# Windowed attention in one kernel with experts: softmax on merged blocks of 32 keys, and the weights split into an older block and a masked difference

## The chip, the cores and the metric

One core of a Trainium2 chip runs the whole program. The metric is the device time of one execution in microseconds, the median over runs. A profiled execution comes with its own time, which is its span in the trace plus a little around it.

## What is computed

```python
x  = L0_attn_x                       # (16, 256, 128), float32
xn = layernorm(x)
x  = x + attn_layer(xn) + experts(xn)

# attn_layer: 16 heads of 8, 4 key/value heads, window of 32
h = layernorm(x) * g1 + b1
q, k, v = h @ Wq + bq, h @ Wk + bk, h @ Wv + bv      # k, v repeated 4 times
q, k = rope(q), rope(k)
scores = einsum('bhqd,bhkd->bhqk', q, k) / sqrt(8)
valid  = (col <= row) & (row - col < 32)
attn   = softmax(where(valid, scores, -1e9))
out    = einsum('bhqk,bhkd->bhqd', attn, v)
x  = x + (out @ Wo + bo)
return x + gelu(layernorm(x) @ Wf1 + bf1) @ Wf2 + bf2   # with g2, b2

# experts: 8 of them, two for each token, hidden width 448
# inter = silu(x @ w1) * (x @ w3) * gate;  y = inter @ w2
```

## The kernel before

Every engine has its own program, written out in order; semaphores join them. A batch is 256 tokens, two tiles of 128. There are 16 batches and 8 blocks of 32 queries in each. `step(k)` of an engine holds what it does while batch k is in its scores: scores and shifted exponent for batch k, transposed weights, attend and norm for batch k-1, projection, residual and statistics for k-2, `h2` (the input of the feed-forward part) for k-3, and heads, keys and queries for k+1.

The program has four stretches. After normalisation and routing come the seven **lead steps** k = 0 to 6, in which POOL also issues 64 indirect DMAs that scatter the rows to the experts' slots, and VectorE also adds the bias and rotates queries and keys of batch k+2 (`add_bias`, `rotate`). Then come eight **expert steps** k = 7 to 14, each with nine expert tiles of 128 slots; here POOL does bias and rotation, and scatters each tile's result (`scatter_y`). A tile goes through `transpose_xs` (split), `take_xsT` on VectorE, `up_products` (seven products, 14 records in the trace, since a float32 product shows as two), `silu` on ACT, `gated` on VectorE (pair, L722, and two products, L728 and L730), `down_product` (four products) and `take_y` on ACT. `tile_up(i)` and `tile_down(i-1)` frame one slot of the order in which the attention work of TensorE stands. The up products of the next tile need the gate of the one before, since a tile uses the only pair of banks; a down product also waits for the split after the next. Last come step 15 and three more, in which the feed-forward part (`up`, `gelu`, `down`) and the sums of expert results (`add_experts`) run, with `resid` on POOL, and a tail of down products.

Scores of a batch before: four units of two blocks (`scores`, L1048 and L1053). Each block of 32 queries is multiplied with 64 keys, the older block and its own. Row partitions are (head of a group, query), columns (block, group g, keys). A bf16 product of the identity with a table of 0 and -1e30 puts the mask into PSUM first. `shift` takes the maximum out of PSUM (L650) and writes the difference to `S` (L657), `exps` works on all of `S` (L906), `weights_T` transposes a unit (L667), and `attend` (L1074) multiplies weights and values of both blocks, with four more columns for the sum. `norm` divides and transposes (L672 to L679). `newer`, `dv` and `pO` don't exist yet.

Other lines of the text: L894 and L900 take keys and queries to SBUF, L279 to L297 are bias and rotation, L412 and L415 the root for `h2` on POOL, L483 and L487 `resid` on POOL, L702 is `h2` on VectorE, L740 `add_experts`, L855 an early copy of 512 PSUM columns by ACT, L592 an early product of 512 columns on VectorE.

## Time and profile before

| | us |
|---|---|
| runs, median (lowest to highest) | 540.97 (540.45 to 542.07) |
| the profiled execution | 541.51 |
| its span | 539.6 |
| TensorE busy, products | 461.3 (85%) |
| VectorE busy | 380.3 (70%) |
| POOL busy | 252.5 (47%) |
| ACT busy | 232.4 (43%) |

A product's end is modelled, so starts are safer than ends on TensorE. The stretches by time: routing to about 54 us, lead steps to about 166, expert steps to about 452, the rest to 539.6. PE is TensorE's products, PEld its weight loads, DVE is VectorE.

### The profile page before, as it was taken

What the parts mean: (1) busy time and instruction counts of PE and PEld (TensorE: products, weight loads), DVE (VectorE), ACT (ScalarE), POOL (GpSimd) and SP (SyncE); (2) the same over time, 40 slices, a digit from 0 to 9 for tenths busy, and PEclk for the clock granted to TensorE, in tenths of its full rate; (3) what the DMA queues carried; (4) which work ended last, traced back from release to release, by engine and by line L of the source; (5) the groups of instructions that cost most, each with busy time, mean ns of one, the idle gap of its engine ahead of it and who ended that gap; (6) DMA issues with size and microseconds to landing.
All of it is one profiled execution on the core that took longest, in us unless ns stands there. A gap on an engine that the chain in (4) does not pass through costs nothing.

```text
span 539.6 us, 11287 instructions
## 1 busy us (share of the span) xinstructions
PE 461.3 (85%) x3102; PEld 408.8 (76%) x3103; DVE 380.3 (70%) x1132; ACT 232.4 (43%) x487; POOL 252.5 (47%) x373
## 2 busy tenths in 40 slices
PE   3921687898778999999999999999999998999967
PEld 2810476686668898888888998998988996675657
DVE  6868989779975847758578477584784753447784
ACT  2692433233251454445524544545335455454310
POOL 4626776744650734636437346363462425412520
PEclk9975777768777999999999999999999999999979
DMA  8961411100111455545544555454544540403042
GB/s 220 326 259 35 157 49 41 35 26 30 36 30 44 139 167 144 155 143 140 163 141 132 162 150 155 138 160 148 152 152 136 171 134 7 151 1 97 22 117 79
DMA packets 40571, 63.96 MB, mean 119 GB/s; under 512 B 6718, under 2 KB 27074, under 8 KB 40400
## 3 DMA queue, kind: packets, MB, share of 16 engines
q1 hardware_dynamic: 35456, 54.65, 33.3%
q0 software_dynamic: 4352, 8.47, 4.8%
q8 instruction: 23, 0.38, 0.3%
q10 hardware_dynamic: 720, 0.30, 0.3%
q14 instruction: 20, 0.16, 0.1%
HBM read 48.05 MB, written 15.87 MB: 118 GB/s over the span
## 4 chain that ended last, share of the span: by engine, by line
PE 57%; DVE 22%; issue 11%; ACT 8%; POOL 1%; DMA 1%; DVEq 0%; ACTq 0%; POOLq 0%
PE bank L1112 13%; PE bank L1074 11%; PE bank L1125 9%; PE bank L1053 6%; PE bank L1150 5%; PE bank L1139 4%; DVE rmax L650 3%; DVE pT L667 3%; DVE S L657 2%; PE bank L1086 2%; ACT L906 2%; DVE x_sb L740 2%; PE bank L1048 1%; DVE h L702 1%; ACT act L915 1%
## 5 line engine op out<-in xcount | busy, mean ns | idle before, releaser
L1112 PE MATMUL bank<-xsT,w_sb 128*128 128x128 f32 x1008 | 128.2, 279 | 4.4 <-DVE inter L730 2.7
L1112 PEld LDWEIGHTS bank<-xsT,w_sb 128*128 128x128 f32 x1008 | 119.5, 194 | 7.6 <-issue 5.4
L431 POOL DMA_INDIRECT scratch_ys<-ysb,pair x72 | 71.8, 997 | 36.1 <-issue 24.8
L1074 PEld LDWEIGHTS bank<-vbd,pT 128*128 128x128 f32 x512 | 73.7, 225 | 13.2 <-DVE pT L667 6.9
L1125 PE MATMUL bank<-w_sb,inter 128*128 x576 | 80.2, 282 | 4.1 <-issue 2.0
L1074 PE MATMUL bank<-vbd,pT 128*128 128x36 f32 x512 | 74.6, 303 | 10.3 <-DVE pT L667 9.2
L1125 PEld LDWEIGHTS bank<-w_sb,inter 128*128 128x128 f32 x576 | 71.8, 192 | 8.5 <-issue 7.0
L421 POOL DMA_INDIRECT scratch_xs<-xn_sb,slot x64 | 63.2, 988 | 31.5 <-issue 17.9
L243 POOL TENSOR_TENSOR spare_sb<-eps_sb 128x1 f32<-128x1 f32 x87 | 16.7, 192 | 128.0 <-ACT ysb L921 127.7
L1053 PE MATMUL bank<-kT,qbd 128*128 128x256 f32 x256 | 72.5, 410 | 0.0
L921 ACT ACTIVATE ysb<-bank 128x128 f32<-128x128 f32 x72 | 19.8, 275 | 114.8 <-PE bank L1125 114.8
L714 DVE COPY xsT<-bank 128x128 f32<-128x128 f32 x72 | 20.6, 286 | 67.2 <-PE bank L1101 66.9
L1053 PEld LDWEIGHTS bank<-kT,qbd 128*128 128x128 f32 x256 | 54.0, 211 | 8.8 <-issue 0.9
L650 DVE TENSOR_REDUCE rmax<-bank 128x4 f32<-128x256 f32 x128 | 47.0, 407 | 17.5 <-PE bank L1053 17.5
L657 DVE TENSOR_TENSOR S<-bank,rmax 128x256 f32<-128x256 f32 x128 | 48.3, 419 | 3.3
L667 DVE STREAM_TRANSPOSE pT<-S 128x512 f32<-128x512 f32 x64 | 44.4, 696 | 0.0
L894 ACT ACTIVATE kT<-bank 32x256 f32<-32x256 f32 x64 | 23.9, 373 | 41.7 <-PE bank L1037 41.2
L730 DVE TENSOR_TENSOR inter<-bank,act 128x384 f32<-128x384 f32 x72 | 40.1, 557 | 1.0
L906 ACT ACTIVATE S<-S 128x2048 f32<-128x2048 f32 x16 | 30.6, 1911 | 21.5 <-DVE S L657 21.4
L1048 PE MATMUL bank<-maskb_sb,identb_sb 128*128 128x512 bf16 x64 | 27.0, 422 | 11.7 <-DVE S L657 7.5
L1150 PEld LDWEIGHTS bank<-wf_sb,gT_sb 128*128 128x128 f32 x256 | 32.1, 207 | 5.9 <-issue 5.9
L914 ACT ACTIVATE act<-bank 64x128 f32<-64x128 f32 x72 | 19.3, 268 | 39.7 <-PE bank L1112 39.1
(136 smaller groups left out, 692.9 us busy)
## 6 DMA issues: line engine op xcount, KB each, us to landing
w_sb<-in_w SPq DMA_DIRECT2D x72, 448.0 KB, 3.3
scratch_xs<-blank_sb SPq DMA_DIRECT2D x9, 520.0 KB, 6.0
xsb<-scratch_xs SPq DMA_DIRECT2D x72, 65.0 KB, 1.8
w_sb<-scratch_ys SPq DMA_DIRECT2D x8, 512.0 KB, 5.2
w_sb<-in_w SPq DMA_DIRECT2D x1, 2048.0 KB, 10.9
out_dram<-x_sb SPq DMA_DIRECT2D x8, 256.0 KB, 2.3
scratch_ys<-ysb,pair POOLq DMA_INDIRECT x72, 2.6
scratch_xs<-xn_sb,slot POOLq DMA_INDIRECT x64, 2.3
```

What stands on the lines that cost most here:

```text
L421: nc.gpsimd.indirect_dma_start(xs, bass.IndirectOffsetOnAxis(ap=slot[:, t, c:c + 1], axis=0), xn_sb[:, t, :], None).then_inc(scattered[g], 16)
L431: nc.gpsimd.indirect_dma_start(ys, bass.IndirectOffsetOnAxis(ap=pair[:, i % 3:i % 3 + 1], axis=0), ysb[:, i % 3, :], None, bounds_check=2 ...
L650: last = nc.vector.tensor_reduce(rmax[:, u, n, :], src, AX.XY, ALU.max)
L657: last = nc.vector.tensor_tensor(S[:, u, n * 256:(n + 1) * 256].rearrange("p (h g k) -> p h g k", h=2, k=WIN), bank[u % 2][:, n * 256:(n + ...
L667: nc.vector.transpose(pT[:, 4 * u:4 * u + 4].rearrange("p n g q -> p (n g q)"), S[:, u, :]).then_inc(pT_ready, 1)
L730: nc.vector.tensor_tensor(inter[:, p, 0:FULL], h3_bank[:, 0:FULL], act1[:, p, 0:FULL], ALU.mult).then_inc(inter_ready, 1)
L906: nc.scalar.activation(S, S, ACT.Exp).then_inc(exp_ready, 1)
L1053: last = nc.tensor.matmul(bank[u % 2][:, i * 256:(i + 1) * 256], qbd[:, p, n].rearrange("p h q -> p (h q)"), kT[:, p, :, n * WIN:n * WIN + ...
L1074: last = nc.tensor.matmul(turn_bank[:, n * VW:(n + 1) * VW], pT[:, 2 * n + i].rearrange("p g q -> p (g q)"), vbd[:, p, n + i, :], start=(i ...
L1112: last = nc.tensor.matmul(to[:, c % EC * P:(c % EC + 1) * P], w13_sb[:, i % 3, c * P:(c + 1) * P], xsT[:, p, :], start=True, stop=True)
L1125: last = nc.tensor.matmul(y_bank[:, 0:D], inter[:, p, c * P:(c + 1) * P], w2_sb[:, ds(at + c * P, P)], start=(c == 0), stop=(c == EC - 1))
L1150: last = nc.tensor.matmul(bank[6 + i % 2][:, t * D:(t + 1) * D], gT[i % 4][:, c, t * P:(t + 1) * P], wf2_sb[:, c, :], start=(c == 0), stop ...
```

## The change

For each query 32 of the 64 keys are valid: of column j, the older block's key if j is above the query's place in its block, and the block's own key otherwise. The new kernel computes both blocks' scores for half a batch (four blocks) apart, own keys into bank 0 and older keys into bank 1, without a mask product; block 0 gets -1e30 as its older scores from one bf16 product. ACT copies the own scores to `S` (`keep_own`), VectorE copies older scores over them where the table `older` says so (`copy_predicated`), and takes maximum and difference in `S`. `S`, the exponential and the transposed weights `pT` are half as wide. For the values, each weight belongs to one of two keys: `attend` applies all weights to the older block's values and the weights times `newer` (`pO`, by `newer_part`) to the difference of own and older values (`dv`, by `value_steps`). `newer_part` runs on VectorE for batches 0 to 5 and on POOL after that, `value_steps` always on POOL. POOL's loop holds two steps in a turn in place of one, since the halves of the buffers alternate. POOL's bias and rotation stand behind one more scatter.

```diff
+        def in_lead(b):
+            return isinstance(b, int) and b < LEAD - 1
+        def part_count(b):
+            return (pO_ready_dve, b + 1) if in_lead(b) else (pO_ready, b + 2 - LEAD)
+        def newer_part(ops, eng, b):
+            ready = pO_ready_dve if in_lead(b) else pO_ready
+            eng.wait_ge(pT_ready, 2 * b + 2)
+            if some(b):
+                eng.wait_ge(pv_psum, b)
+            ops.tensor_tensor(pO.rearrange("p n g q -> p (n g) q"), pT.rearrange("p n g q -> p (n g) q"),
+                              bc(newer_sb.rearrange("p (a q) -> p a q", a=1), [P, NBLK * G, WIN]), ALU.mult).then_inc(ready, 1)
...
+            def value_steps(b, p):
+                pool.wait_ge(vbd_ready, b + 1)
+                if some(b - 1):
+                    pool.wait_ge(pv_psum, b - 1)
+                nc.gpsimd.tensor_tensor(dv[:, p, :, 0:NKV * HD], vbd[:, p, 1:NBLK + 1, 0:NKV * HD],
+                                        vbd[:, p, 0:NBLK, 0:NKV * HD], ALU.subtract).then_inc(dv_ready, 1)
...
+                if exists(k - 1) and not in_lead(k - 1):
+                    newer_part(nc.gpsimd, pool, k - 1)
                 if group is not None:
                     scatter(group, (0, 1))
                 tiles((0,))
...
                 if group is not None:
                     scatter(group, (2, 3))
                 tiles((1,))
+                if exists(k):
+                    value_steps(k, p)
+                tiles((2,))
                 if exists(k + 2) and not early(k + 2):
                     add_bias(nc.gpsimd, pool, k + 2)
                     rotate(nc.gpsimd, pool, k + 2)
-                tiles((2, 3, 4, 5, 6, 7))
+                tiles((3, 4, 5, 6, 7))
...
-            def shift(b, u):
-                dve.wait_ge(scores_psum, UNITS * b + u + 1)
...
-                last.then_inc(shifted, 1)
-            def weights_T(b, u):
+            def shift(b, h):
+                row = "p (a k) -> p a k"
+                half = S[:, h].rearrange(row, k=WIN)
+                dve.wait_ge(own_kept, 2 * b + h + 1)
+                wait_apart_dve("older_psum", older_psum, 2 * b + h + 1)
+                nc.vector.copy_predicated(half, bc(older_sb.rearrange("p (a k) -> p a k", a=1), [P, HALF * G, WIN]),
+                                          bank[1].rearrange(row, k=WIN)).then_inc(chosen, 1)
+                dve.wait_ge(chosen, 2 * b + h + 1)
+                nc.vector.tensor_reduce(rmax[:, h], half, AX.X, ALU.max).then_inc(rowmax_ready, 1)
+                dve.wait_ge(rowmax_ready, 2 * b + h + 1)
+                nc.vector.tensor_tensor(half, half, bc(rmax[:, h].rearrange("p (a k) -> p a k", k=1), [P, HALF * G, WIN]),
+                                        ALU.subtract).then_inc(shifted, 1)
+            def weights_T(b, h):
                 dve.wait_ge(exp_ready, b + 1)
                 if some(b):
                     dve.wait_ge(pv_psum, b)
-                nc.vector.transpose(pT[:, 4 * u:4 * u + 4].rearrange("p n g q -> p (n g q)"), S[:, u, :]).then_inc(pT_ready, 1)
+                    semaphore, value = part_count(b - 1)
+                    dve.wait_ge(semaphore, value)
+                nc.vector.transpose(pT[:, HALF * h:HALF * h + HALF].rearrange("p n g q -> p (n g q)"), S[:, h]).then_inc(pT_ready, 1)
...
+                    weights_T(k - 1, 1)
+                    if in_lead(k - 1):
+                        newer_part(nc.vector, dve, k - 1)
                 tile_split(2)
                 tile_gated(1)
-                if exists(k - 1):
-                    weights_T(k - 1, 1)
                 if exists(k):
                     values(k, p)
                 if exists(k + 1):
...
                 tile_split(3)
                 tile_gated(2)
                 if exists(k):
-                    shift(k, 1)
-                if exists(k - 1):
-                    weights_T(k - 1, 2)
+                    shift(k, 0)
                 tile_split(4)
                 tile_gated(3)
                 if exists(k - 3):
                     h2_of(k - 3)
-                if exists(k):
-                    shift(k, 2)
-                if exists(k - 1):
-                    weights_T(k - 1, 3)
                 tile_split(5)
                 tile_gated(4)
                 if exists(k):
-                    shift(k, 3)
+                    shift(k, 1)
...
+            def keep_own(b, h):
+                act.wait_ge(own_psum, 2 * b + h + 1)
+                if some(b):
+                    act.wait_ge(pT_ready, 2 * b)
+                nc.scalar.activation(S[:, h], bank[0], ACT.Copy).then_inc(own_kept, 1)
             def exps(b):
-                act.wait_ge(shifted, UNITS * b + UNITS)
+                act.wait_ge(shifted, 2 * b + 2)
                 nc.scalar.activation(S, S, ACT.Exp).then_inc(exp_ready, 1)
...
                 products(-1)
+                if exists(k):
+                    keep_own(k, 0)
                 gates(1)
                 products(0)
...
                 products(2)
+                if exists(k):
+                    keep_own(k, 1)
                 gates(4)
                 products(3)
...
-            def scores(b, p, u):
-                if u == 0:
+            def own_scores(b, p, h):
+                if h == 0:
                     pe.wait_ge(qbd_ready, b + 1)
                     pe.wait_ge(kT_ready, b + 1)
...
-                last.then_inc(scores_psum, 1)
+                if some(2 * b + h):
+                    pe.wait_ge(own_kept, 2 * b + h)
+                for i in range(HALF):
+                    n = HALF * h + i
+                    last = nc.tensor.matmul(bank[0][:, i * GW:(i + 1) * GW], qbd[:, p, n].rearrange("p h q -> p (h q)"),
+                                            kT[:, p, :, (n + 1) * WIN:(n + 2) * WIN], start=True, stop=True)
+                last.then_inc(own_psum, 1)
+            def older_scores(b, p, h):
+                if some(2 * b + h):
+                    pe.wait_ge(chosen, 2 * b + h)
+                for i in range(HALF):
+                    n = HALF * h + i
+                    if n == 0:
+                        last = nc.tensor.matmul(bank[1][:, 0:GW], identb_sb, neg_sb, start=True, stop=True)
+                    else:
+                        last = nc.tensor.matmul(bank[1][:, i * GW:(i + 1) * GW], qbd[:, p, n].rearrange("p h q -> p (h q)"),
+                                                kT[:, p, :, n * WIN:(n + 1) * WIN], start=True, stop=True)
+                last.then_inc(older_psum, 1)
...
             def attend(b, p, quarter, h2T_out):
                 if quarter == 0:
-                    pe.wait_ge(pT_ready, UNITS * b + UNITS)
-                    pe.wait_ge(vbd_ready, b + 1)
+                    semaphore, value = part_count(b)
+                    pe.wait_ge(semaphore, value)
+                    pe.wait_ge(dv_ready, b + 1)
                     if some(h2T_out):
                         pe.wait_ge(h2T_ready, h2T_out)
                 for n in range(quarter * NBLK // 4, (quarter + 1) * NBLK // 4):
-                    for i in range(2):
-                        last = nc.tensor.matmul(turn_bank[:, n * VW:(n + 1) * VW],
-                                                pT[:, 2 * n + i].rearrange("p g q -> p (g q)"),
-                                                vbd[:, p, n + i, :], start=(i == 0), stop=(i == 1))
+                    to = turn_bank[:, n * VW:(n + 1) * VW]
+                    if n > 0:
+                        nc.tensor.matmul(to, pT[:, n].rearrange("p g q -> p (g q)"), vbd[:, p, n, :], start=True, stop=False)
+                    last = nc.tensor.matmul(to, pO[:, n].rearrange("p g q -> p (g q)"), dv[:, p, n, :], start=(n == 0), stop=True)
                 if quarter == 3:
...
-                    scores(k, p, 0)
+                    own_scores(k, p, 0)
                 tile_down(-1)
                 tile_up(1)
                 if exists(k + 1):
...
                 tile_down(0)
                 tile_up(2)
                 if exists(k):
-                    scores(k, p, 1)
+                    older_scores(k, p, 0)
                 tile_down(1)
                 tile_up(3)
                 if exists(k):
-                    scores(k, p, 2)
+                    own_scores(k, p, 1)
                 tile_down(2)
                 tile_up(4)
                 if exists(k):
-                    scores(k, p, 3)
+                    older_scores(k, p, 1)
...
-    q, k = (p % WIN)[:, None], np.arange(KW)[None, :]
-    valid = (k - WIN <= q) & (k > q)
-    allowed = np.repeat(valid[:, None, :], NBLK, 1)
-    allowed[:, 0, :WIN] = False
-    maskadd = np.where(allowed, 0.0, NEG).reshape(P, -1).astype(f32)
+    older = (np.arange(WIN)[None, :] > (p % WIN)[:, None]).astype(np.int32)
+    newer = (np.arange(WIN)[None, :] >= (p % WIN)[:, None]).astype(f32)
```

VectorE, one lead step, from the norm of the batch before to the second (before) or last (after) shift. Before:

```order
L667 STREAM_TRANSPOSE pT<-S 128x512
L650 TENSOR_REDUCE rmax<-bank 128x4 x2
L657 TENSOR_TENSOR S<-bank,rmax 128x256 x2
L667 STREAM_TRANSPOSE pT<-S 128x512
L641 TENSOR_TENSOR vbd<-vt,vmask_sb 128x8x32
L540 STREAM_TRANSPOSE vt<-bank 128x256
L650 TENSOR_REDUCE rmax<-bank 128x4 x2
L657 TENSOR_TENSOR S<-bank,rmax 128x256 x2
L667 STREAM_TRANSPOSE pT<-S 128x512
L702 TENSOR_SCALAR h<-xn_sb,mv,rstd 128x128 x2
L650 TENSOR_REDUCE rmax<-bank 128x4 x2
L657 TENSOR_TENSOR S<-bank,rmax 128x256 x2
```

After:

```order
L704 STREAM_TRANSPOSE pT<-S 128x512 x2
L292 TENSOR_TENSOR pO<-pT,newer_sb 128x1024
L680 TENSOR_TENSOR vbd<-vt,vmask_sb 128x8x32
L577 STREAM_TRANSPOSE vt<-bank 128x256
L245 MEMSET spare_sb 128x1
L690 COPY_PREDICATED S<-older_sb,bank 128x512
L693 TENSOR_REDUCE rmax<-S 128x16
L695 TENSOR_TENSOR S<-S,rmax 128x512
L739 TENSOR_SCALAR h<-xn_sb,mv,rstd 128x128 x2
L245 MEMSET spare_sb 128x1
L690 COPY_PREDICATED S<-older_sb,bank 128x512
L693 TENSOR_REDUCE rmax<-S 128x16
```

Both transposes now stand in a row at the head, the product with `newer` behind them, and the shifts are two groups of copy, maximum and difference in place of four pairs.

ACT, head of the expert loop's first step (two tiles: SiLU of tile 0, take_y of the last tile, SiLU of tile 1). Before:

```order
L914 ACTIVATE act<-bank 64x128
L915 ACTIVATE act<-bank 128x384
L920 ISA
L921 ACTIVATE ysb<-bank 128x128
L911 REGISTER_ALU
L914 ACTIVATE act<-bank 64x128
L915 ACTIVATE act<-bank 128x384
L920 REGISTER_ALU
L921 ACTIVATE ysb<-bank 128x128
```

After:

```order
L952 ACTIVATE act<-bank 64x128
L953 ACTIVATE act<-bank 128x384
L958 ISA
L959 ACTIVATE ysb<-bank 128x128
L937 ISA
L940 ACTIVATE S<-bank 128x512
L949 REGISTER_ALU
L952 ACTIVATE act<-bank 64x128
L953 ACTIVATE act<-bank 128x384
```

The copy of the own scores (L940) stands between the first tile's result and the second tile's SiLU.

POOL, head of the same step: scatter of the last tile, scatter of tile 0, then the root for h2. Before:

```order
L243 TENSOR_TENSOR spare_sb<-eps_sb 128x1
L431 DMA scratch_ys<-ysb,pair 8192x128
L429 REGISTER_ALU
L243 TENSOR_TENSOR spare_sb<-eps_sb 128x1
L431 DMA scratch_ys<-ysb,pair 8192x128
L411 ISA
L412 TENSOR_TENSOR ve<-mv,eps_sb 128x2
L413 REGISTER_ALU
L415 TENSOR_TENSOR rstd<-ve,nhalf_sb 128x2
```

After:

```order
L249 TENSOR_TENSOR spare_sb<-eps_sb 128x1
L454 DMA scratch_ys<-ysb,pair 8192x128
L289 ISA
L292 TENSOR_TENSOR pO<-pT,newer_sb 128x1024
L452 REGISTER_ALU
L249 TENSOR_TENSOR spare_sb<-eps_sb 128x1
L454 DMA scratch_ys<-ysb,pair 8192x128
L434 ISA
L435 TENSOR_TENSOR ve<-mv,eps_sb 128x2
L436 REGISTER_ALU
L438 TENSOR_TENSOR rstd<-ve,nhalf_sb 128x2
```

The product with `newer` (L292) stands ahead of tile 0's scatter and of the root.

## Rows read from the trace of the kernel before

**Rows 1.** The page, part 4: the chain that ended last, by engine.

```profile
PE 57%; DVE 22%; issue 11%; ACT 8%; POOL 1%; DMA 1%; DVEq 0%; ACTq 0%; POOLq 0%
```

**Rows 2.** Busy time by stretch, one in the lead, one in the expert steps.

```profile
92.00:109.00 17.00, 14.43 (x64) 12.49 (x64) 13.85 (x41) 5.38 (x10) 9.72 (x12) 0.70 0.10 32
...
250.00:286.00 36.00, 33.96 (x270) 31.71 (x270) 24.19 (x71) 17.11 (x39) 16.86 (x29) 1.00 0.50 148
```

**Rows 3.** Groups by line and shape: busy us, mean ns, idle before.

```profile
L657 DVE TENSOR_TENSOR S<-bank,rmax 128x256 f32<-128x256 f32 x128 | 48.3, 419 | 3.3
...
L650 DVE TENSOR_REDUCE rmax<-bank 128x4 f32<-128x256 f32 x128 | 47.0, 407 | 17.5 <-PE bank L1053 17.5
...
L667 DVE STREAM_TRANSPOSE pT<-S 128x512 f32<-128x512 f32 x64 | 44.4, 696 | 0.0
...
L906 ACT ACTIVATE S<-S 128x2048 f32<-128x2048 f32 x16 | 30.6, 1911 | 21.5 <-DVE S L657 21.4
...
L592 DVE TENSOR_TENSOR h2T_sb<-h2T_sb 128x512 f32<-128x512 f32 x1 | 0.7, 691 | 0.0
...
L483 POOL TENSOR_TENSOR x_sb<-x_sb,bf_sb 128x512 f32<-128x512 f32 x8 | 10.3, 1288 | 0.0
...
L855 ACT ACTIVATE xnT<-bank 128x512 f32<-128x512 f32 x8 | 4.8, 600 | 3.8 <-PE bank L996 3.8
```

**Rows 4.** Timeline, lead steps: start, us, engine, line, operation.

```profile
67.58 0.70 DVE L667 STREAM_TRANSPOSE pT<-S 128x512 f32<-128x512 f32 x1
...
99.22 0.67 DVE L667 STREAM_TRANSPOSE pT<-S 128x512 f32<-128x512 f32 x1
...
102.98 1.57 ACT L900 ACTIVATE qbd<-bank,qmask_sb 128x256 f32<-128x256 f32 x4
...
107.82 3.22 PE L1074 MATMUL bank<-vbd,pT 128*128 128x36 f32 x16 [1.56 <-DVE pT L667]
...
116.57 0.67 DVE L667 STREAM_TRANSPOSE pT<-S 128x512 f32<-128x512 f32 x1
...
131.49 0.67 DVE L667 STREAM_TRANSPOSE pT<-S 128x512 f32<-128x512 f32 x1
...
165.24 0.45 DVE L679 STREAM_TRANSPOSE outT<-on 128x256 f32<-128x256 f32 x1
```

**Rows 5.** Timeline of one expert step, 250 to 287 us.

```profile
252.04 0.38 PE L1048 MATMUL bank<-maskb_sb,identb_sb 128*128 128x512 bf16 x1
...
252.45 0.87 POOL L279 TENSOR_TENSOR qkb<-gT_sb,bqkv_sb 128x320 f32<-128x320 f32 x1
...
252.52 0.83 DVE L722 SCALAR_TENSOR_TENSOR pair<-xsb,slotgrid_sb 128x1 int32<-128x1 f32 x1
...
253.12 1.05 PE L1125 MATMUL bank<-w_sb,inter 128*128 x8
...
254.36 1.64 PEld L1112 LDWEIGHTS bank<-xsT,w_sb 128*128 128x128 f32 x14 [0.38 <-issue]
...
257.75 0.20 DVE L722 SCALAR_TENSOR_TENSOR pair<-xsb,slotgrid_sb 128x1 int32<-128x1 f32 x1
...
258.96 1.64 PEld L1112 LDWEIGHTS bank<-xsT,w_sb 128*128 128x128 f32 x14
...
265.82 1.91 ACT L906 ACTIVATE S<-S 128x2048 f32<-128x2048 f32 x1
...
266.02 1.64 PEld L1112 LDWEIGHTS bank<-xsT,w_sb 128*128 128x128 f32 x14
...
271.12 1.64 PEld L1112 LDWEIGHTS bank<-xsT,w_sb 128*128 128x128 f32 x14
```

**Rows 6.** The chain in order of time: start us, us, what.

```profile
198.24 0.97 PE bank L1125 x8
...
447.16 0.97 PE bank L1125 x8
```

**Rows 7.** Timeline, the step after the last batch.

```profile
487.83 0.63 DVE L702 TENSOR_SCALAR h<-xn_sb,mv,rstd 128x128 f32<-128x128 f32 x2
```

93 lines of the change are left out of this document (40 added, 53 removed).

## The prediction, made before the change was run

> **What bounds the kernel now.** The chain that ended last comes first: TensorE holds 57% of it and VectorE 22% [rows 1], so two kinds of stretch have to be told apart. The busy table by stretch does that [rows 2]. From 92 to 109 us, in the seven lead steps, VectorE works 13.9 of 17 us at a TensorE clock of 0.70. From 250 to 286 us, in the eight steps that also run nine expert tiles each, TensorE is busy 34 of 36 us at full clock (the 2.4 GHz level). The lead is paced by VectorE with waits of VectorE and TensorE on each other; the expert steps are paced by TensorE, with gaps where it waits for what ACT and VectorE make of each tile.
>
> A lead step in order of time [rows 4]: the first weight transpose of a step starts at 99.22 and that of the next at 116.57, 17.35 us. TensorE can't begin to apply the weights (attend, L1074) before the fourth transpose, at 107.82, which is 8.6 us into the step; once begun, norm, the last VectorE work of the step, waits for it. Six such steps, from 67.58 to the end of the last output transpose at 165.69, take 98.1 us, 16.4 each. They differ with TensorE's clock: attend's first 16 records take 3.22 us at 107.82, at the low level, and the step after 116.57, with the clock risen in its second half, takes 14.92 in place of 17.35.
>
> Expert steps: from 198.24 to 447.16 seven of them pass, 35.6 us each [rows 6]. Inside one, the starts of the up products of following tiles lie 4.60 us apart at 254.36 and 258.96, and 5.10 apart at 266.02 and 271.12 [rows 5]. Work alone doesn't fill these: 14 records of up take 1.64 us, so one record of 128 columns costs 0.117; up, down, split and eight more records are 31, or 3.6 us. In the first of these intervals VectorE is late: shifts, transposes and h2 stand between the gates, and a scalar_tensor_tensor on 128x1 takes 0.83 us at 252.52 beside POOL's L279. In the second ACT is late: the exponential on 2048 columns runs from 265.82 for 1.91 us, between two table loads, and the SiLU of the tile stands behind it.
>
> **The change, part by part.** *Scores on TensorE.* Before, a unit is one mask product on 512 bf16 columns and two products on 256; it starts at 252.04 and the next work at 253.12, so four units cost 4.32 us a batch. After, 15 products on 128 columns are 30 records, 3.5 us, and one bf16 product about 0.1. Attend goes from 16 products to 15, 0.23 less. Together 0.95 us a batch, where TensorE is the bound.
>
> *VectorE's softmax.* Before, by the means [rows 3], eight maxima at 0.407, eight subtractions at 0.419 and four transposes at 0.696 are 9.4 us. After, two predicated copies, two maxima and two subtractions on 512 columns, and two transposes. No row shows a predicated copy. The nearest rows are the 512 column products, 0.69 (L592), for two streams that are each read once; the far end is four passes, 2.8 us. I take 0.69, because mask and data are again two streams and the kept value is not needed. The maximum on 512 comes by the same slope to 0.68. That is 2 x (0.69 + 0.68 + 0.69) + 2 x 0.70 = 5.5 us. Three operations that follow each other by a semaphore, and one memset for the wait, give back about 0.2 each half.
>
> *The masked part of the weights.* 1024 columns on VectorE in the lead: from 0.419 at 256 and 0.691 at 512 it is 1.2 us. On POOL, where 512 columns take 1.29 (L483), 2.4 to 2.6 us. *Value steps*, 256 columns on POOL, half of L483, about 0.7.
>
> *ACT.* Two new copies of 512 PSUM columns at 0.60 (L855) are 1.2 us; the exponential halves from 1.91 to about 1.05. Work is even, but it moves out of the place where it hurts.
>
> **Lead steps.** VectorE saves 9.4 - 5.5 - 1.2 - 0.4 = 2.3 us by the means; single pairs before overlap a little, so I take 1.9. The path says the same: attend no longer waits for four transposes mixed with shifts but for both transposes at the step's start, the mask product, and h2, which TensorE transposes first: 1.4 + 1.2 + 0.85 for values and their transpose + 2.2 for one shift + 0.6 for h2 + 0.5 to TensorE's transpose is about 6.8, against 8.6. Second shift, bias, rotation, residual and norm follow as before. Six steps at 1.9 are 11, and the first step, with shifts only, 1; together 12 us. The new ACT copy of the second half stands behind keys and queries (each as long as the 1.57 us at 102.98) and ends at about 5.8, before VectorE wants it at 6.3. POOL works 9.7 us in 17 and gets 0.7 more; with the pauses between its scatters that is some 13 and stays below the 14.5 that remain. Bounds: if all six steps find the low clock, they take 6 x (17.35 - 1.9) = 93, and 5 + 1 = 6 us are gained; if all find the high one, 14.92 - 1.9 = 13.0, of which VectorE's own work, now without a wait, gives back up to 0.5, and the gain is 18 us.
>
> **Expert steps.** Interval by interval. (a) The three that hold scores in front of a down product get 0.14 shorter each by records, 0.5 us, of which 0.2 are hidden where ACT's keys and queries hold the SiLU. (b) The interval of 4.60: after the gate only h2 is left on VectorE, and POOL's rotation, moved behind one more scatter, doesn't meet h2 any more; TensorE's own work is 3.6 + 0.25, so 0.75 goes. (c) The interval before it loses one transpose and one shift of two, 0.3. (d) The interval of 5.10 is set by ACT and loses what the exponential loses, 0.86. (e) Where attend has three products instead of four, VectorE's chain takes over, 0.1. The sum is 2.3. Against it stand meetings with POOL: the subtraction now has both inputs in SBUF, as the pair instruction (L722) has, and stands next to POOL's rotation. The 0.83 us at 252.52, against 0.20 for the same instruction at 257.75, show the price of one meeting, 0.6; half of it a step, 0.3. So 2.0 us, eight steps, 16 us. The new wait in ACT's queue (copy of the first half, behind both transposes, ahead of the second tile's SiLU) costs 0.1 to 0.7 on ACT; heads and a down product on TensorE cover it, with about 0.3 to spare. POOL's 2.5 us product ends some ten microseconds before attend asks for it. The values product on VectorE may wait for it about 1.9 us, and the wait for the next split covers that. Bounds: 0.7 a step, when only the TensorE records are saved and some of them are lost again, 6 us; 3 a step, 24.
>
> By the Trainium skill (SBUF — State Buffer, Who interferes with whom) a VectorE instruction with two SBUF inputs and a GpSimd instruction that reads SBUF exclude each other for a whole instruction. By that rule the trace agrees: the instruction of 252.52 ends at 253.35 and POOL's L279 at 253.32 [rows 5]. The rule speaks against this change, since POOL's new product is 2.5 us long; the first rival works that out from rows.
>
> **Tail.** The last batch's scores and the weights of the batch before save 1.1 us, and the exponential 0.9. But in the step after the last batch POOL has the mask product ahead of rstd, and h2 waits for rstd. Before, h2 starts at 487.83 [rows 7]; now it stands behind transposes that end near 486.5, 2.5 of product and about 0.9 of rstd, at 489.9, 2.1 late, which eats the 2.0; 1 more for POOL's product meeting the expert sums on VectorE. Net +1, from -2 to +3.
>
> **Sum.** The profiled execution took 541.5 us (span 539.6), the median of the runs is 540.97. 541.5 - 12 - 16 + 1 = 514.5. All parts at their poor ends give 541.5 - 6 - 6 + 3 = 532.5, all at their good ends 541.5 - 18 - 24 - 2 = 497.5; they rarely fall so together, and the forecast's own range is 503 to 528.
>
> **Rivals.** *Meetings with POOL eat the expert steps.* POOL now has 3.2 us more of SBUF reads a step, one of them 2.5 us long; if VectorE's values, pair or subtraction stand behind it and the next gate is late, each step loses 1 to 2 us of its 2.3. For it: 252.52. Against it: the product begins after the scatter of the last tile, when VectorE mostly waits for a split. Expert steps -4, lead -9 and tail +3 give 531.5. *The predicated copy is slow, and the kernel ends slower than before.* Place: in the middle of each shift, 14 times on the lead's VectorE path and 16 times between two gates. Every microsecond over 0.69 costs about 30; from 0.69 + 27/30 = 1.6 us a copy the gain is gone; at four passes, 2.8, the time is 514.5 + 63 = 577. For it: no row. Against it: every VectorE operation in the rows keeps to about 1.06 ns a column. *The lead finds the low clock everywhere*, since TensorE does less work: lead -6 in place of -12, 520.5; inside the forecast's range. *More than forecast*: all lead steps at the high clock and 3 us an expert step give 541.5 - 18 - 24 + 1 = 500. *The change saves TensorE nothing*, because narrow products cost as much as wide ones: against it, 14 records of 128 columns take 1.64 us, and a unit with four records on 256 takes 1.08 with its mask.
>
> **How the numbers follow.** Forecast with the low clock case inside 0.68, meetings with POOL 0.20, slow copy 0.07, more than forecast 0.05. The predicted time is 514.5. The range 501 to 532 takes in the case of POOL's meetings, and leaves out the slow copy, the most of the more-than-forecast case and the edges of the others, somewhat under 2 in 10. A measurement of this kernel tells a change from none at about 0.3%, 1.6 us. Faster: the three cases under 533 and their edges, 0.91; the same 0.02; slower: 0.07.
>
> **What would show it.** Right: COPY_PREDICATED near 0.7 us; lead steps of 14 to 15.5 us; expert steps near 33.6; the exponential near 1.05 and the interval across it near 4.2; gaps of TensorE behind VectorE's gates smaller. Wrong: a copy above 1.6 us; the second tile's SiLU waiting for the first copy of S; VectorE's values, pair or subtraction of 2 us beside POOL's product; attend waiting for POOL; lead steps that stay at 16 us with VectorE idle before norm.

## The result, and the profile after

The kernel got slower. Four runs of the changed kernel have a median of 557.7 us (551.89 to 560.54), those of the kernel before beside them 540.71 (539.51 to 542.07): a ratio of 1.028, interval 1.019 to 1.037. Ratios and their intervals, here and below, are of fast executions alone (here 560.54 is left out as slow), so they differ a little from the quotients of the medians. The forecast was 514.5, the range 501 to 532.

The profiled execution took 551.89 us, the fastest of the four, with a span of 550.0. From the page of the changed kernel, its engines and its chain by engine, which answer to [rows 1]:

```profile
span 550.0 us, 11471 instructions
...
PE 448.4 (82%) x3246; PEld 411.2 (75%) x3247; DVE 370.1 (67%) x979; ACT 236.0 (43%) x519; POOL 303.7 (55%) x401
...
PE 49%; DVE 23%; issue 13%; POOL 7%; DMA 5%; ACT 2%; DVEq 0%; POOLq 0%; ACTq 0%
```

TensorE's share of the chain fell from 57% to 49%, and two names that had 1% each hold 12% now: POOL and a DMA. The groups of the changed kernel by line and shape (columns as in [rows 3]):

```profile
L759 DVE SCALAR_TENSOR_TENSOR pair<-xsb,slotgrid_sb 128x1 int32<-128x1 f32 x72 | 44.0, 611 | 13.6 <-DMA scratch_ys<-ysb,pair 13.4
...
L695 DVE TENSOR_TENSOR S<-S,rmax 128x512 f32<-128x512 f32 x32 | 24.2, 757 | 1.1
L292 POOL TENSOR_TENSOR pO<-pT,newer_sb 128x1024 f32<-128x1024 f32 x10 | 23.6, 2359 | 26.1 <-DVE pT L704 25.9
L690 DVE COPY_PREDICATED S<-older_sb,bank 128x512 f32<-128x512 int32 x32 | 23.3, 729 | 19.8 <-PE bank L1104 19.2 <-issue 0.6
L693 DVE TENSOR_REDUCE rmax<-S 128x16 f32<-128x512 f32 x32 | 22.0, 686 | 1.1
L704 DVE STREAM_TRANSPOSE pT<-S 128x512 f32<-128x512 f32 x32 | 20.5, 679 | 0.0
L940 ACT ACTIVATE S<-bank 128x512 f32<-128x512 f32 x32 | 19.2, 600 | 45.8 <-DVE pT L704 43.0 <-PE bank L1091 2.7
...
L944 ACT ACTIVATE S<-S 128x1024 f32<-128x1024 f32 x16 | 16.9, 1057 | 11.9 <-DVE S L695 11.8
```

Every new operation costs about what the prediction gave it: predicated copy 0.729 us (0.69 forecast), maximum 0.686 (0.68), subtraction 0.757 (0.69), GpSimd's product 2.36, exponential 1.06. What stands out is the first row. The pair instruction works on one column a partition and takes 0.20 us when nothing disturbs it; its mean is now 0.61, over 72 of them, and before it 13.6 us are spent on a DMA that nobody waited for before, but once for 0.6 us.

By stretch, from the timelines of the two profiled executions: the first up product of the expert steps starts at 155.19 (165.92 before), 10.7 earlier; from there to the start of the last down product are 302.2 us (286.2), 16.0 more; from there to the end 92.6 (87.5), 5.1 more. The sum is +10.4, and 541.5 + 10.4 is 551.9.

Inside an expert step, the starts of the up products of its nine tiles (0 to 8) cut it into nine intervals. I read the starts from TensorE's timeline and took means over six steps, the second to the seventh. This ruler serves for every kernel below (us; those left out stay within 0.5 of each other):

```
kernel                                1-2   3-4   4-5   5-6   6-7   7-8   step  low clock
before                                3.70  4.16  4.59  3.64  3.47  5.14  35.83   0
after                                 5.81  3.94  3.89  3.71  5.40  4.22  37.87   3
rot_back                              5.81  3.95  3.75  5.66  4.14  4.31  38.24   3
mask_dve                              3.74  4.00  4.00  3.71  5.46  4.80  36.74   4
both                                  3.77  5.11  3.75  4.78  4.07  4.11  36.59   2
pieces                                3.79  4.08  3.93  3.70  5.26  4.70  36.41   2
before_load                           5.43  4.36  4.59  3.72  3.47  5.14  37.69   0
before_load4                          3.68  4.07  4.61  3.72  3.47  5.12  35.82   0
pieces_late                           3.80  4.82  3.75  3.91  3.80  4.20  35.22   1
dve_late                              3.77  4.95  3.75  3.55  3.58  4.21  34.86   0
dve_rot2                              3.78  3.53  4.31  3.70  5.24  4.83  36.40   3
dve_split                             3.78  4.85  4.25  3.40  3.56  4.21  35.12   0
whole_late                            5.81  4.64  3.75  5.23  4.53  4.43  39.28   4
before_rot                            3.68  3.72  4.31  3.53  5.25  4.25  35.89   2
```

The last column counts the places in all eight expert steps where the granted clock fell, the low clock with which the first step begins in every kernel aside. In the kernel before there are none. The second row against the first is the result in one line: 4-5 and 7-8 lost 0.70 and 0.92 as forecast, and 1-2 and 6-7 gained 2.11 and 1.93.

**The interval 1-2: VectorE held by GpSimd.** Timeline of the changed kernel, 198.5 to 203 us:

```profile
198.64 2.78 DVE L759 SCALAR_TENSOR_TENSOR pair<-xsb,slotgrid_sb 128x1 int32<-128x1 f32 x1
199.03 2.36 POOL L292 TENSOR_TENSOR pO<-pT,newer_sb 128x1024 f32<-128x1024 f32 x1
201.45 0.29 DVE L765 TENSOR_TENSOR inter<-bank,act 64x128 f32<-64x128 f32 x1
201.75 0.56 DVE L767 TENSOR_TENSOR inter<-bank,act 128x384 f32<-128x384 f32 x1
...
202.46 0.79 PE L1163 MATMUL bank<-xsT,w_sb 128*128 128x128 f32 x5 [1.89 <-DVE inter L767]
```

The pair instruction of tile 1, 0.20 us of work, ends at 201.42, and GpSimd's product at 201.39. The gate stands behind it in VectorE's queue and TensorE behind the gate: 1.89 us idle here, 0.92 in the first step and 1.9 to 2.4 in the others.

**The interval 6-7: a scatter that leaves late.** The same kernel, 211 to 224 us:

```profile
211.75 0.89 POOL L300 TENSOR_TENSOR qkb<-gT_sb,bqkv_sb 128x320 f32<-128x320 f32 x1
...
213.88 0.28 ACT L959 ACTIVATE ysb<-bank 128x128 f32<-128x128 f32 x1 [2.10 <-PE bank L1176]
...
216.31 0.72 POOL L318 TENSOR_TENSOR kr<-ra,rb 128x256 f32<-128x256 f32 x1
...
217.34 1.01 POOL L454 DMA_INDIRECT scratch_ys<-ysb,pair  x1 [0.15 <-POOL spare_sb L249]
...
217.77 0.33 SPq L351 DMA_DIRECT2D w_sb<-in_w  x1
...
221.70 0.22 DVE L759 SCALAR_TENSOR_TENSOR pair<-xsb,slotgrid_sb 128x1 int32<-128x1 f32 x1 [2.05 <-DMA scratch_ys<-ysb,pair]
...
222.96 1.24 PE L1163 MATMUL bank<-xsT,w_sb 128*128 128x128 f32 x9 [1.86 <-DVE inter L767]
```

The result of tile 3 is ready at 214.16, but GpSimd is in bias and rotation until 217.03, which now stand behind the scatter of tile 2; the scatter goes out at 217.34. The pair of tile 6 uses the same of three buffers and must wait for it to land; it starts 4.36 us after the issue. VectorE waits 2.05, TensorE 1.86. The wait has two parts: the scatter leaves late, and it also takes 4.2 us to land, where the scatters of this kernel take a median of 2.8. The row of L351, a load of weights on SyncE's queue, comes back under whole_late.

**The clock.** Busy time by stretch of the changed kernel (columns as in [rows 2]), two steps, and three pieces of 4 us in the second:

```profile
230.46:268.05 37.59, 32.96 (x283) 31.85 (x281) 24.19 (x60) 17.25 (x41) 21.18 (x31) 1.00 0.50 142
268.05:308.96 40.91, 36.23 (x283) 34.70 (x281) 24.16 (x60) 17.27 (x41) 20.66 (x31) 0.92 0.44 129
...
274.00:278.00 4.00, 2.02 (x15) 1.60 (x14) 3.89 (x5) 1.83 (x6) 3.71 (x4) 1.00 0.21 78
278.00:282.00 4.00, 3.89 (x23) 3.85 (x24) 1.98 (x6) 0.78 (x3) 1.39 (x3) 0.65 0.49 148
282.00:286.00 4.00, 4.00 (x35) 4.00 (x35) 2.76 (x8) 2.50 (x7) 1.66 (x3) 0.93 0.42 131
```

TensorE is busy 2.02 of 4 us before 278, where the pair of tile 1 is held, and then the granted clock is 0.65: part of the stretch at the 1.2 GHz level. The step with two such falls has the same records and takes 3.3 us more than its neighbour. Not every wait of 1.9 us is followed by a fall.

**The tail.** Timeline of the changed kernel, the step after the last batch, against [rows 7]:

```profile
491.45 2.34 POOL L292 TENSOR_TENSOR pO<-pT,newer_sb 128x1024 f32<-128x1024 f32 x1 [17.82 <-DVE pT L704]
493.75 0.19 POOL L435 TENSOR_TENSOR ve<-mv,eps_sb 128x2 f32<-128x2 f32 x1
494.02 0.71 POOL L438 TENSOR_TENSOR rstd<-ve,nhalf_sb 128x2 f32<-128x2 f32 x1
494.76 2.06 DVE L739 TENSOR_SCALAR h<-xn_sb,mv,rstd 128x128 f32<-128x128 f32 x2 [3.39 <-POOL rstd L438]
...
496.93 0.66 PE L1113 MATMUL bank<-ident_sb,h 128*128 128x128 f32 x2 [4.97 <-issue]
```

`h2` starts 37.4 us after the last down product of the expert steps (35.8 before), takes 2.06 in place of 0.63 beside GpSimd's next products, and TensorE stands idle for 4.97 us. The clock follows. Busy time by stretch, the 20 us that begin 30 us after that last down product, in the changed kernel and then in the kernel before:

```profile
487.35:507.35 20.00, 14.28 (x51) 8.30 (x50) 11.14 (x29) 7.63 (x11) 6.45 (x7) 0.74 0.23 66
```

```profile
482.07:502.07 20.00, 18.89 (x107) 13.57 (x106) 13.84 (x46) 9.21 (x12) 5.01 (x8) 0.91 0.25 78
```

TensorE gets 51 records through in place of 107, at a granted clock of 0.74 in place of 0.91.

By the Trainium skill (SBUF — State Buffer, Who interferes with whom) a VectorE instruction with two SBUF inputs contends with a GpSimd instruction that reads SBUF, and whichever comes first holds the shared ports for its whole length while the other waits. The trace agrees on the length: 2.78 us of the pair beside 2.36 of the product, with ends 0.03 apart. It doesn't agree on the order, as far as recorded starts tell: the pair's begins 0.39 us ahead of the product's, and the pair is the one that waits.

### The profile page after: what moved, and what is told of

Read it like the earlier page. It is cut to its first block, busy times and chain, and to the rows that moved or that the text cites. A ratio compares the mean times of both kernels' runs of the same rounds, so it can differ in the third digit from the quotient of the medians.

```text
span 550.0 us, 11471 instructions
## 1 busy us (share of the span) xinstructions
PE 448.4 (82%) x3246; PEld 411.2 (75%) x3247; DVE 370.1 (67%) x979; ACT 236.0 (43%) x519; POOL 303.7 (55%) x401
## 4 chain that ended last, share of the span: by engine, by line
PE 49%; DVE 23%; issue 13%; POOL 7%; DMA 5%; ACT 2%; DVEq 0%; POOLq 0%; ACTq 0%
PE bank L1163 15%; PE bank L1176 7%; DMA scratch_ys<-ysb,pair 5%; PE bank L1201 5%; PE bank L1127 4%; PE bank L1190 4%; PE bank L1126 3%; PE bank L1091 3%; PE bank L1104 3%; DVE inter L767 2%; DVE pT L704 2%; DVE x_sb L777 2%; PE bank L1137 2%; DVE S L690 1%; DVE xn_sb L560 1%
## 5 line engine op out<-in xcount | busy, mean ns | idle before, releaser
L1127 PE MATMUL bank<-dv,pO 128*128 128x36 f32 x256 | 54.6, 299 | 3.7 <-ACT h2T_sb L917 3.7
L759 DVE SCALAR_TENSOR_TENSOR pair<-xsb,slotgrid_sb 128x1 int32<-128x1 f32 x72 | 44.0, 611 | 13.6 <-DMA scratch_ys<-ysb,pair 13.4
L1127 PEld LDWEIGHTS bank<-dv,pO 128*128 128x128 f32 x256 | 44.6, 218 | 5.4 <-issue 5.4
L1091 PE MATMUL bank<-kT,qbd 128*128 128x128 f32 x256 | 41.8, 316 | 5.3 <-ACT qbd L932 3.5
L1126 PE MATMUL bank<-vbd,pT 128*128 128x36 f32 x224 | 45.9, 291 | 0.0
L1091 PEld LDWEIGHTS bank<-kT,qbd 128*128 128x128 f32 x256 | 38.2, 228 | 7.6 <-issue 7.1
L1126 PEld LDWEIGHTS bank<-vbd,pT 128*128 128x128 f32 x224 | 39.2, 218 | 1.1 <-issue 1.0
L940 ACT ACTIVATE S<-bank 128x512 f32<-128x512 f32 x32 | 19.2, 600 | 45.8 <-DVE pT L704 43.0
L292 POOL TENSOR_TENSOR pO<-pT,newer_sb 128x1024 f32<-128x1024 f32 x10 | 23.6, 2359 | 26.1 <-DVE pT L704 25.9
L690 DVE COPY_PREDICATED S<-older_sb,bank 128x512 f32<-128x512 int32 x32 | 23.3, 729 | 19.8 <-PE bank L1104 19.2
L1104 PE MATMUL bank<-kT,qbd 128*128 128x128 f32 x224 | 35.4, 303 | 1.4 <-DVE S L690 1.4
```

The lines of the kernel that those rows point to most:

```text
L690: nc.vector.copy_predicated(half, bc(older_sb.rearrange("p (a k) -> p a k", a=1), [P, HALF * G, WIN]), bank[1].rearrange(row, k=WIN)).then ...
L759: nc.vector.scalar_tensor_tensor(pair[:, b:b + 1], xsb[:, b, D + 1:XW], slotgrid_sb[:, ds(j, 1)], xsb[:, b, D:D + 1], ALU.is_equal, ALU.ad ...
L1091: last = nc.tensor.matmul(bank[0][:, i * GW:(i + 1) * GW], qbd[:, p, n].rearrange("p h q -> p (h q)"), kT[:, p, :, (n + 1) * WIN:(n + 2) * ...
L1104: last = nc.tensor.matmul(bank[1][:, i * GW:(i + 1) * GW], qbd[:, p, n].rearrange("p h q -> p (h q)"), kT[:, p, :, n * WIN:(n + 1) * WIN], ...
L1126: nc.tensor.matmul(to, pT[:, n].rearrange("p g q -> p (g q)"), vbd[:, p, n, :], start=True, stop=False)
L1127: last = nc.tensor.matmul(to, pO[:, n].rearrange("p g q -> p (g q)"), dv[:, p, n, :], start=(n == 0), stop=True)
```

## The experiments

All ratios are against runs of the kernel before on the same chip. Four kernels first undo one thing of the change each.

**rot_back.** The rotation goes back to its old place, value steps before it.

```diff
                 if exists(k):
                     value_steps(k, p)
-                tiles((2,))
                 if exists(k + 2) and not early(k + 2):
                     add_bias(nc.gpsimd, pool, k + 2)
                     rotate(nc.gpsimd, pool, k + 2)
-                tiles((3, 4, 5, 6, 7))
+                tiles((2, 3, 4, 5, 6, 7))
```

> The changed kernel with one thing undone: POOL's bias and rotation stand again ahead of the scatter of tile 2. Theory A (two new waits cost the expert steps, POOL's product with newer and the late scatter of tile 3): the wait of VectorE's pair instruction for the DMA of scratch_ys, 13.4 us in the changed kernel, falls under 3 us; TensorE's gap of 1.9 us before the up product of tile 8 goes; 8 x 1.9 less, some 535 to 548 us. Rival (the scatter's place doesn't matter, the waits come from the halves of S and ACT's queue): within 2 us of the changed kernel.

556.84 us median, ratio 1.028 (1.020 to 1.036): nothing gained, a miss. The number is the one that the rival named, but its mechanism (halves of `S`, ACT's queue) isn't in the trace. The ruler says why nothing was gained: the wait didn't go, it moved from 6-7 to 5-6 (5.66). Now the scatter of tile 2 stands behind 0.75 us of value steps and 4.9 of bias and rotation. The pair of tile 5 asks for it 1.1 us after its issue and waits 1.8 to 3.3 us. Before, with the rotation alone in that place, the margin had been just enough.

**mask_dve.** The product for the masked part on VectorE for all batches.

```diff
         def in_lead(b):
-            return isinstance(b, int) and b < LEAD - 1
+            return True
```

> The changed kernel with the product with newer on VectorE for all batches, nothing else moved. Theory A: pair (L759) beside that product falls from 2.6 to 0.2 us, TensorE's gap of 1.9 us before the up product of tile 2 falls under 0.5 since 1.2 us of VectorE work take its place; 8 x 1.4 less in the expert steps and about 4 less after the last batch, where POOL's root for h2 waited: 536 to 545 us. Rival (POOL's extra work as such is what costs, by late scatters): the DMA wait would shrink and the gap before tile 2 stay.

537.06 us (534.63 to 538.22), ratio 0.989 (0.981 to 0.996). Interval 1-2 is 3.74 again. VectorE does 1.22 us more a step, and the kernel is 20 us faster than with that work on GpSimd.

**both.** Both edits together.

> Both edits: rotation ahead of tile 2's scatter, product with newer on VectorE. Theory A: the expert steps come near the 33.6 us of the prediction plus what 1.2 us of VectorE work cost, and the time is 515 to 530 us, faster than the kernel before. If one wait only hides behind the other, the sum of the two single gains isn't reached and the time stays above 535.

538.58 us (530.46 to 541.49), ratio 0.996 (0.992 to 1.000): a miss by 9 us, with the wait again in 5-6. What came is the other branch of the expectation, one wait behind the other and a time above 535. The profiled execution, 528.6 of span, was the fastest; it has two falls of the clock and a mean granted clock of 0.910; the two slowest, 541.0 and 541.5, have 0.896. So the spread of this kernel goes with the clock.

**pieces.** The product stays on GpSimd, cut in four.

```diff
-            ops.tensor_tensor(pO.rearrange("p n g q -> p (n g) q"), ...
+            pieces = 1 if in_lead(b) else 4
+            step = NBLK // pieces
+            for i in range(pieces):
+                at = slice(i * step, (i + 1) * step)
+                last = ops.tensor_tensor(pO[:, at].rearrange("p n g q -> p (n g) q"), ...
+            last.then_inc(ready, 1)
```

> The changed kernel with POOL's product with newer in four pieces of 256 columns in place of one of 1024, same place, somewhat more POOL time (4 x 0.72 against 2.36). Theory A with an exclusive hold for one instruction: pair waits for one piece only, 0.9 us in place of 2.6, and TensorE's gap before tile 2 falls from 1.9 to about 0.3: 8 x 1.4 less, 539 to 548 us. Rival (VectorE is slowed for as long as POOL works, whatever the pieces): no change, 550 to 560.

537.24 us (535.68 to 539.05), ratio 0.989 (0.982 to 0.997). GpSimd works more (2.8 to 3.0 us in place of 2.36), and 20 us are gone all the same. So it isn't GpSimd's work that costs, but that it comes in one long instruction. The gain is even larger than expected. The pair was to wait for one piece, 0.9 us; it takes 0.82 in the last two steps, but only 0.21 to 0.48 in the second to the sixth. In the second it begins 0.39 us ahead of the first piece, as far as it began ahead of the whole product in the rows above, and here it isn't held to the piece's end. Why the same head start helps against the short instruction and not against the long one stays open.

Then the same from the other side: the kernel before, with idle work added.

**before_load.** In each expert step GpSimd multiplies 1024 columns that nobody reads.

```diff
                 if some(0 if m is None else m):
                     tiles((-1,))
+                if m is not None:
+                    pool.wait_ge(pT_ready, UNITS * (k - 1) + 1)
+                    nc.gpsimd.tensor_tensor(loadB, loadA, loadA, ALU.mult)
```

> The kernel before, with one idle product added to GpSimd in each expert step: 1024 columns f32, SBUF to SBUF, after the scatter of the last tile of the step before, waiting for the first weight transpose as the new mask product does. Nobody reads its result. Theory A (an SBUF instruction of GpSimd holds back VectorE's instructions with two SBUF inputs, the pair above all, until it ends): the pair instruction there takes over 2 us, TensorE waits about 1.9 us a step, and the low clock follows in some steps: 15 to 22 us in all, 555 to 563. Rival B (the price in the changed kernel came from its other waits, and the product alone is covered): 540 to 543.

556.31 us (554.13 to 557.96), ratio 1.026 (1.021 to 1.032). The timeline, 244 to 256 us:

```profile
248.46 2.34 DVE L728 SCALAR_TENSOR_TENSOR pair<-xsb,slotgrid_sb 128x1 int32<-128x1 f32 x1
248.86 1.91 POOL L456 TENSOR_TENSOR loadB<-loadA 128x1024 f32<-128x1024 f32 x1
...
251.84 1.80 PE L1118 MATMUL bank<-xsT,w_sb 128*128 128x128 f32 x14 [1.43 <-DVE inter L736]
```

The same picture as in the changed kernel, alone: interval 1-2 is 5.43 in place of 3.70, the step 1.9 us longer, and the clock stays full in the second to the eighth step. One idle instruction a step on an engine that is busy half of the time costs 13.5 us.

**before_load4.** The same work in four instructions of 256 columns.

```diff
-                    nc.gpsimd.tensor_tensor(loadB, loadA, loadA, ALU.mult)
+                    for at in range(0, 1024, 256):
+                        nc.gpsimd.tensor_tensor(loadB[:, at:at + 256], loadA[:, at:at + 256], loadA[:, at:at + 256], ALU.mult)
```

> The same idle product cut into four of 256 columns, about 0.72 us each, 2.9 us in all on GpSimd. Theory A: the pair waits for one piece at most, 0.7 us a step in place of 2: 541 to 547. If it is GpSimd's time as such that costs (its scatter comes later by the sum), it is as slow as the product in one piece or slower.

542.59 us, ratio 1.001 (0.995 to 1.007). No difference. The timeline, 236 to 250 us:

```profile
240.73 0.47 DVE L729 SCALAR_TENSOR_TENSOR pair<-xsb,slotgrid_sb 128x1 int32<-128x1 f32 x1
241.24 2.52 POOL L457 TENSOR_TENSOR loadB<-loadA 128x256 f32<-128x256 f32 x4
241.54 0.56 DVE L737 TENSOR_TENSOR inter<-bank,act 128x384 f32<-128x384 f32 x1
```

2.5 us on GpSimd cost nothing; 1.9 us in one instruction cost 13.5. The pair ends at 241.20, just ahead of the first piece, so here no piece holds it. The gate (L737) has one input in PSUM and runs at 0.56 in the midst of them.

Next, the second cause: value steps and rotation apart.

**pieces_late.** Rotation at its old place, value steps behind the scatter of tile 5, product in pieces.

```diff
                 tiles((1,))
-                if exists(k):
+                if m is None and exists(k):
                     value_steps(k, p)
                 ...
                     rotate(nc.gpsimd, pool, k + 2)
-                tiles((2, 3, 4, 5, 6, 7))
+                tiles((2, 3, 4, 5))
+                if m is not None and exists(k):
+                    value_steps(k, p)
+                tiles((6, 7))
```

> The changed kernel with GpSimd's mask product in four pieces (537.2 before), the rotation ahead of the scatter of tile 2 again, and the value steps moved from ahead of the rotation to behind the scatter of tile 5, in the expert steps. Theory C (what is left in each step is one wait of 1.3 to 2.2 us of the pair for a scatter that GpSimd issues late, because value steps and rotation together, or the rotation one tile later, stand ahead of it; the kernel before has a margin of under 0.75 us there): the wait goes, 1.5 to 2 us a step, and with it the low clock of single stretches: 518 to 526. Rival D (the scatters fly longer for another reason, traffic of the weight loads): 535 to 539.

532.14 us (526.35 to 540.43), ratio 0.978 (0.970 to 0.986), a miss by 6 us. The ruler shows the DMA's wait gone from four steps of six, with 3.3 in 5-6, and still there in two (5.18 and 4.95); theory C is right as far as it goes, but the margin is not safe.

**dve_late.** The same with the product on VectorE.

> The same with the mask product in one piece on VectorE. Theory C: 516 to 525. Rival D: 535 to 539, as the kernel with the product on VectorE and the rotation moved back had it (538.6).

519.24 us (518.23 to 520.71), ratio 0.958 (0.953 to 0.963). A hit, and the fastest kernel of all: 38 us less than the changed one with the same arithmetic. TensorE's waits for the gate are mostly gone and no expert step behind the first has a low clock:

```profile
PE 442.0 (86%) x3246; PEld 405.7 (79%) x3247; DVE 370.3 (72%) x989; ACT 236.0 (46%) x519; POOL 284.1 (55%) x391
...
PE 63%; DVE 18%; issue 8%; ACT 5%; DMA 3%; POOL 1%; DVEq 0%; POOLq 0%; ACTq 0%
```

(Page of dve_late, engines and chain.) Against both, it moves nothing but the value steps, 0.75 us a step, to where GpSimd waits anyway; that is worth 19 us.

**dve_rot2.** As dve_late, but the rotation where the change had put it, behind the scatter of tile 2.

> As the kernel at 519.2 (product on VectorE, value steps behind the scatter of tile 5), but with the rotation behind the scatter of tile 2, where the change had put it. It differs from the kernel at 537.1 by the place of the value steps alone. Theory C1 (the rotation one scatter later is enough to make a scatter late): the interval of the up products of tiles 6 and 7 is again near 5.4 us in place of 3.5, while the interval of 4.95 before h2 shrinks by about 1; a step of 35.8 to 36.7, and the low clock in some: 527 to 537. Rival C2 (it takes rotation and value steps together): 513 to 518, better than 519.2, since the rotation no longer meets h2.

537.54 us (530.11 to 541.65), ratio 0.989 (0.983 to 0.995), half a microsecond above the expected range. The intervals are those of C1: 6-7 is 5.24, while 3-4 fell to 3.53. The rotation's place alone makes the scatter of tile 3 late.

**dve_split.** As dve_late, but bias sums behind tile 1 and the rotation proper behind tile 2.

> As the kernel at 519.2, but the bias sums (1.6 us on GpSimd) stay behind the scatter of tile 1 and the rotation proper (3.1 us) goes behind that of tile 2, so that GpSimd never works more than about 3 us between two scatters. If a late scatter is the cause, each is late by under 1.5 us and no pair waits for one; the interval of 4.95 shrinks too: 511 to 518. If a DMA wait shows again, 520 to 530.

530.17 us (528.05 to 532.02), ratio 0.979 (0.973 to 0.984), a miss. In the expert steps three pairs wait for a scatter, 1.2 us in all (1.9 in dve_late), and a step is 35.12, but 3-4 keeps its 4.85 and 4-5 gets 0.5 longer. The profiled execution is 13.7 us longer than that of dve_late: 6.9 of it in the lead, though nothing in its code differs, 2.5 in the expert steps and 4.3 in the tail. In the lead's last step stands (timeline, 144 to 152 us):

```profile
145.54 3.56 DVE L743 TENSOR_SCALAR h<-xn_sb,mv,rstd 128x128 f32<-128x128 f32 x2
145.87 0.74 POOL L470 TENSOR_TENSOR dv<-vbd 128x256 f32<-128x256 f32 x1
146.55 0.86 POOL L300 TENSOR_TENSOR qkb<-gT_sb,bqkv_sb 128x320 f32<-128x320 f32 x1
147.36 0.72 POOL L302 TENSOR_TENSOR vb<-gT_sb,bqkv_sb 128x256 f32<-128x256 f32 x1
```

0.6 us of `h2` take 3.56 beside a row of GpSimd's products, and TensorE waits 4.00 for it. I know of no reason why this meeting happened there and not in dve_late, other than the time at which each engine came; it was not tested. Leads of the same code do differ: the four traces with the lead of the kernel before end it at 161.6 to 168.0, the ten with the new one at 152.4 to 159.6.

**whole_late.** As dve_late, but with the product whole on GpSimd: only the first cause.

> As the kernel at 519.2, but with the mask product whole on GpSimd from the expert steps on, as the change has it; so the changed kernel with only the second cause (scatters) taken away. By the run of the kernel before with an idle product (+13.5) and the later h2 after the last batch (+2): 533 to 541, the interval of the up products of tiles 1 and 2 near 5.8 us. If the two causes add in full as the numbers of single edits say (557.7 less 537.1 is 20.6), 538 to 542; if it stays near 557, the scatters were never a cause.

561.1 us (558.91 to 563.41), ratio 1.037 (1.030 to 1.044), slower than the changed kernel and a miss by 20 us. The first cause stands at 5.81 as expected, but the second is back without being asked for: 5-6 is 5.23. The two share a margin: the time between the issue of tile 2's scatter and the pair of tile 5, which asks for its buffer. The rows, whole_late first, dve_late second (L351 is a load of 448 KB of weights for a later tile):

```profile
298.34 1.01 POOL L454 DMA_INDIRECT scratch_ys<-ysb,pair  x1
...
298.92 0.33 SPq L351 DMA_DIRECT2D w_sb<-in_w  x1
...
302.61 0.22 DVE L761 SCALAR_TENSOR_TENSOR pair<-xsb,slotgrid_sb 128x1 int32<-128x1 f32 x1 [1.66 <-DMA scratch_ys<-ysb,pair]
```

```profile
278.93 1.01 POOL L454 DMA_INDIRECT scratch_ys<-ysb,pair  x1
...
280.19 0.34 SPq L351 DMA_DIRECT2D w_sb<-in_w  x1
...
282.13 0.21 DVE L761 SCALAR_TENSOR_TENSOR pair<-xsb,slotgrid_sb 128x1 int32<-128x1 f32 x1
```

In dve_late the pair comes 3.20 us after the issue and finds the buffer free; in the kernel before 3.48 (221.81 and 225.29). In whole_late it asks 2.61 after, in both 2.60 (209.99, and 215.22 less a wait of 2.63), and the pair of tile 6 in the changed kernel 2.31, and each time it waits, until 4.3 to 5.2 us after the issue. It asks earlier in whole_late because the held pair of tile 1 pushes the tiles together behind it: the results of tiles 1 and 2 come 3.50 us apart, in dve_late 4.98, while the rotation between their scatters stays as long.

Asking 0.6 us earlier isn't enough for such a wait. In dve_late this scatter lands 2.28 us after its issue, and a pair that asked at 2.6 would find it there. In whole_late it lands after 4.07. What goes with the longer flight is the load of weights: its issue comes 0.58 us behind the scatter's in whole_late and 0.43 in the changed kernel, but 1.26 in dve_late. In the second to seventh expert steps of all fourteen traces, 59 scatters have such a load 0.3 to 0.65 us behind them and land after a median of 4.07 us; 49 have it 0.85 to 1.6 us behind and land after 2.32. The kernel both shows the two side by side: in four steps the load comes 0.5 behind tile 2's scatter, which lands after 4.2 to 5.0, and in the next two 1.2 behind, and it lands after 2.3 and 3.0. No experiment moved the load alone, and it isn't everything: once in dve_late the load came 1.2 behind and the scatter still took 4.17. So the margin isn't a slope but an edge: where the tiles come some 0.6 us earlier against the scatter, the pair asks earlier and the scatter also lands later.

**before_rot.** The kernel before with the rotation one scatter later, the last part of the change done alone.

```diff
-                tiles((1,))
+                tiles((1, 2))
                 if exists(k + 2) and not early(k + 2):
                     add_bias(nc.gpsimd, pool, k + 2)
                     rotate(nc.gpsimd, pool, k + 2)
-                tiles((2, 3, 4, 5, 6, 7))
+                tiles((3, 4, 5, 6, 7))
```

> The kernel before with one edit of the change alone: GpSimd's bias sums and rotation one scatter later. Theory C1: in each expert step a pair waits for a late scatter, the interval of the up products of tiles 6 and 7 goes from 3.5 to about 5.3; the interval of 4.6 before h2 loses up to 0.7: net 1 us a step and now and then the low clock, 548 to 558. Rival: only the gain, 535 to 540.

546.02 us (540.95 to 547.43), ratio 1.010 (1.006 to 1.013). Slower, less than expected. The wait is there (timeline, 255 to 275 us):

```profile
263.06 1.01 POOL L431 DMA_INDIRECT scratch_ys<-ysb,pair  x1
...
267.34 0.22 DVE L722 SCALAR_TENSOR_TENSOR pair<-xsb,slotgrid_sb 128x1 int32<-128x1 f32 x1 [1.88 <-DMA scratch_ys<-ysb,pair]
...
268.61 1.80 PE L1112 MATMUL bank<-xsT,w_sb 128*128 128x128 f32 x14 [1.69 <-DVE inter L730]
```

But 6-7 grows by 1.78 while 7-8 falls from 5.14 to 4.25 and 3-5 together lose 0.72. While TensorE waits in 6-7, ACT gets through the long exponential for which 7-8 used to wait. In the changed kernel the exponential is short, 7-8 has nothing to give, and the same wait costs its full size. Here it comes to 0.06 a step, and two falls of the clock. This is the profiled execution, with 540.95 us the fastest of ten; eight of the others took 544.7 to 547.4, and what they lost no trace shows.

## Why the prediction was wrong, step by step

**Operations.** Right in the main. The unknown one, the predicated copy, was taken at 0.69 us from the products on 512 columns and took 0.729, the subtraction at 0.69 and took 0.757; the rival that it is slow falls, though its sign was the one that came.

**TensorE's saving.** 0.95 us a batch by records. In full-clock steps TensorE is busy 34.03 us before (238.87 to 274.71) and 32.96 after: 1.07. Right.

**Lead.** Forecast -12, measured -10.7 between the two profiled executions. Right, within its bounds of 6 and 18. The medians of the ten traces with the new lead and the four with the old one (155.2 and 165.7) lie 10.5 apart.

**The gains of an expert step.** Forecast 2.3, by intervals. (b) 0.75: 4-5 lost 0.70. (d) 0.86: 7-8 lost 0.92, and 1.16 in steps at full clock. (c) 0.3: 3-4 lost 0.22. (a), 0.5 less 0.2 hidden, can't be found: 0-1, 1-2 and 2-3 are within 0.1 of before in mask_dve. Take dve_rot2, which has neither the long product nor the early value steps, and put 3.47 for its waiting interval 6-7 and 3.98 for 7-8 at full clock: the step is 33.8, 2.0 less than before and 0.2 from the forecast. That is a sum over steps, and no run has it: dve_late, the fastest, has 34.86, 1.0 less than before, since its 3-4 is 4.95 where dve_rot2 has 3.53. So the gains exist one by one, but only half of them was measured together.

**What stood against them is the step that failed.** "Half of it a step, 0.3" for meetings with POOL. I priced a meeting by [rows 5], 0.6 us beside an instruction of 0.87, and halved it, where the size of the new product said more: in that very row the pair ends 0.03 us after GpSimd's instruction, and the new one is 2.5 us long. And I wrote that a VectorE wait of 1.9 us is possible and "the wait for the next split covers that". It was the right size on the wrong instruction. The product starts when the scatter of the last tile has gone out, and at that moment VectorE is at the pair of tile 1, with the gate behind it; nothing covers a pair. Measured: 2.11 a step, in every step, and 1.73 with idle work in the kernel before. The first rival had this mechanism, 1 to 2 us a step, at 0.20; its time was 531.5, too low by 20 against the profiled execution and by 26 against the median, since it knew neither of the next two.

**The moved rotation had a price of its own that I didn't look for.** I looked at what the rotation would no longer meet (`h2`, right: 4-5) and not at what queues behind it. Scatter 3 goes out 3.2 us after its result is ready and the pair of tile 6 waits: 1.93 a step. With the 2.11 that is 4.0 against gains of 2.3, which is the sign of the result: a step is 2.04 longer, and the forecast had it 2.0 shorter. The prediction had neither this wait nor the row for it: in the kernel before, one pair in 72 waits for a scatter, for 0.6 us. Such a single short wait would have been the sign that the margin is small.

**The clock of the expert steps.** I took it as full, since it was in [rows 2]. It was full in a kernel whose TensorE never paused there for long: its waits for the gate were 0.4 us at most. In the profiled execution its falls cost some 5 us: in the step from 268.05 3.3 of busy time, and 1.4 in the last step. The three executions that weren't profiled took 5 to 9 us longer, at a mean granted clock of 0.887 to 0.896 where the profiled one has 0.897; what they lost besides the clock no trace shows.

**Tail.** Forecast +1, from -2 to +3; measured +5.1. The late start of `h2` was foreseen at 2.1 and came at 1.6. That `h2` itself takes 1.4 longer beside GpSimd, and that the clock falls after the pause, were not.

**The sum.** Lead -10.7 (forecast -12), expert steps +16.0 (-16), tail +5.1 (+1). Expert steps: six of 2.04 are 12.2, the first +0.9, the last, which had been the shortest, +2.9. The two causes can't be priced apart to the microsecond. Taking the first away brings 20 us, taking the second away while the first stays brings nothing, and taking both away 38.

## What to carry to other kernels

An engine with time to spare isn't free: ask what its longest instruction locks, and which instruction of the critical engine stands there at the moment when it starts. Cut long GpSimd instructions, or give 1.2 us of them to the busy engine; both were worth 20 us here. When work is moved past a DMA issue, follow the DMA to the buffer that it frees, read how much margin its next user had, and look which large transfer is issued just behind it. And a wait isn't only its own length: it moves the tiles behind it, can use up the margin of the next wait, and can bring the clock down. A pause just ahead of another one, though, may hide it (before_rot).

## What was new of the hardware

- A VectorE `scalar_tensor_tensor` on one column, with both inputs in SBUF, took 2.78 us beside a GpSimd product of 2.36, and 0.21 without it. A hold isn't limited to one instruction: `h2`, a `tensor_scalar` on 128 columns, twice, took 3.56 us beside four GpSimd products that followed each other. The first of the two took 2.64, from 0.33 us ahead of the first of these products to the end of the third; undisturbed it takes 0.34. With an input in PSUM the gate took its 0.56 in the middle of GpSimd's work.
- 1024 columns on GpSimd took 2.36 us where the second input is a column mask repeated over the blocks, and 1.91 with one plain tensor as both inputs.
- The scatters of 128 rows land a median of 2.4 to 3.0 us after issue, depending on the kernel. Those with a load of 448 KB of weights issued 0.3 to 0.65 us behind them took a median of 4.07, those with the load 0.85 to 1.6 behind 2.32. That the load is the cause is likely from this, but no experiment moved it.
- The granted clock of expert steps fell only in kernels where TensorE paused for 1.7 us or more at a time, in one to four places of an execution. But before_load, with pauses of 1.4 to 1.8 us in seven of eight steps, kept the full clock, so the pause alone doesn't decide.
